# Layer norm sums taken in the eviction and on ScalarE instead of VectorE statistics, in a fused audio tower kernel

## The reference

```python
ewma = (forward EWMA + backward EWMA) / 2 over time, alpha = 0.1
h  = ewma @ tok_W.T + tok_b                      # (16, 750, 256)
xn = layernorm(h)                                # over the 256 features
for l in 0, 1:                                   # a selective scan, 64 states
    delta = softplus(xn @ Wd[l] + bd[l]); u = xn @ Wi[l] + bi[l]
    s_t = exp(-delta * softplus(A_log[l])) * s_(t-1) + delta * u
    xn  = s @ Wo[l] + bo[l] + (last state @ Ws[l] + bs[l])
h  = h + xn
xf = layernorm(h)
h  = h + silu(xf @ Gs.T) * (xf @ Us.T) @ Ds.T                   # shared, 512 hidden
       + sum over 4 of 16 experts, w_e * (silu(xf @ G_e) * (xf @ U_e)) @ D_e   # routed
layernorm(v) = (v - mean(v)) / sqrt(var(v) + 1e-5)
```

## Time and profile before

| | us |
|---|---|
| three runs | 1300.79, 1304.12, 1304.29; median 1304.12 |
| the profiled execution, whole time | 1308.71 |
| its span, first to last instruction | 1306.6 |
| PE busy | 1171.1 (90%) |
| DVE busy | 940.5 (72%) |
| ACT busy | 552.0 (42%) |
| POOL busy | 414.9 (32%) |

### The profile page before, as it was taken

The page is one execution under the profiler, slowest core; times in us unless marked ns, Lnnn a source line. Parts: engine busy times, 40 slices in busy tenths (PEclk is TensorE's granted clock), DMA queues, the critical chain, the costliest instruction groups (busy, mean ns, idle before and its releaser), DMA issues.

```text
span 1306.6 us, 24750 instructions
## 1 busy us (share of the span) xinstructions
PE 1171.1 (90%) x7477; PEld 1055.9 (81%) x7477; DVE 940.5 (72%) x2374; ACT 552.0 (42%) x899; POOL 414.9 (32%) x281
## 2 busy tenths in 40 slices
PE   3548886997999989998999889998999999999997
PEld 3437765876998779987988789977998899889997
DVE  6785898598757985889758985799668855644443
ACT  1423552461354533662355434563455343223332
POOL 2022253134131623134321623153402530353233
PEclk8556886998999999999999999999999999999999
DMA  4130021022022413122131323231221321243331
GB/s 125 33 88 17 24 64 42 28 67 75 17 53 42 104 46 57 38 58 70 31 59 30 97 54 54 42 85 33 42 64 28 94 46 36 52 107 62 54 51 19
DMA packets 88288, 71.48 MB, mean 55 GB/s; under 512 B 39671, under 2 KB 82848, under 8 KB 88168
## 3 DMA queue, kind: packets, MB, share of 16 engines
q1 hardware_dynamic: 58832, 43.30, 12.2%
q0 software_dynamic: 26832, 26.06, 11.9%
q10 hardware_dynamic: 2504, 0.55, 0.2%
HBM read 31.36 MB, written 39.34 MB: 54 GB/s over the span
## 4 chain that ended last, share of the span: by engine, by line
PE 65%; DVE 24%; issue 7%; ACT 2%; POOL 1%; another core or an unknown queue 1%; DMA 1%; DVEq 0%; POOLq 0%; ACTq 0%
PE gu_ps L1692 18%; PE gu_ps L1665 14%; PE d_ps L1768 10%; PE d_ps L1749 8%; PE ch_ps L1642 3%; PE ch_ps L1736 3%; DVE h L1188 2%; PE ch_ps L1573 2%; DVE h L1196 2%; DVE stats L1202 1%; PE ch_ps L1728 1%; DVE gu_ps L1453 1%; PE ch_ps L1603 1%; DVE h L1464 1%; PE ch_ps L1591 1%
## 5 line engine op out<-in xcount | busy, mean ns | idle before, releaser
L804 POOL DMA_INDIRECT out_dram<-block_rows,entry x99 | 158.2, 1598 | 316.4 <-ACT block_rows L944 295.7
L1692 PE MATMUL gu_ps<-gu_hi,bx_hi 128*128 x792 | 236.8, 299 | 3.2 <-issue 2.1
L1692 PE MATMUL gu_ps<-gu_lo,bx_hi 128*128 x792 | 225.7, 285 | 0.0
L1692 PE MATMUL gu_ps<-gu_hi,bx_lo 128*128 x792 | 225.7, 285 | 0.0
L932 ACT ACTIVATE hid<-gu_ps 128x512 f32<-128x512 f32 (+1 forms) x195 | 115.0, 592 | 253.9 <-PE gu_ps L1692 120.8
L785 POOL DMA_INDIRECT lists<-records,pos x96 | 135.6, 1412 | 204.1 <-DVE pos L1361 178.3
L1749 PE MATMUL d_ps<-down,hid 128*125 128x256 f32 x768 | 186.0, 386 | 0.0
L1692 PEld LDWEIGHTS gu_ps<-gu_hi,bx_hi 128*128 128x128 f32 x792 | 152.5, 193 | 9.5 <-issue 8.6
L1749 PEld LDWEIGHTS d_ps<-down,hid 128*125 128x125 f32 x768 | 141.5, 192 | 19.5 <-issue 0.3
L1692 PEld LDWEIGHTS gu_ps<-gu_hi,bx_lo 128*128 128x128 f32 x792 | 152.6, 193 | 0.9
L1692 PEld LDWEIGHTS gu_ps<-gu_lo,bx_hi 128*128 128x128 f32 x792 | 151.9, 192 | 0.0
(11 more groups left out here) (279 smaller groups left out, 2866.3 us busy)
## 6 DMA issues: line engine op xcount, KB each, us to landing
block_rows<-lists SPq DMA_DIRECT2D x99, 128.0 KB
out_dram<-h SPq DMA_DIRECT2D x24, 500.0 KB
t<-rstd_scratch SPq DMA_DIRECT2D x21, 250.0 KB, 5.4
x_in<-in_x_dram SPq DMA_DIRECT2D x8, 375.0 KB, 7.5
zt<-in_x_dram SPq DMA_DIRECT2D x7, 375.0 KB
entry<-lists SPq DMA_DIRECT2D x99, 8.0 KB, 3.2
out_dram<-block_rows,entry POOLq DMA_INDIRECT x99
lists<-records,pos POOLq DMA_INDIRECT x96
```

What stands on the lines that cost most here:

```text
L804: pool.indirect_dma_start(out=out_rows[0:there, :], out_offset=bass.IndirectOffsetOnAxis(entry[n % UE][:, ID:ID + 1].bitcast(U32), 0), in_ ...
L1692: last = pe.matmul(gu_ps[:, 2 * (g % 2) + half, q * GH:(q + 1) * GH], a[n % 2][:, k, :], w[:, k, bass.ds(of, 1), half * GH:(half + 1) * GH ...
```

## The change

- `tok` and `y`: in place of one `tensor_tensor` of 512 columns and two `bn_stats`, DVE issues two `scalar_tensor_tensor` of 256 columns, each with `accum_out` into `hsum`, the row sums of its tile.
- New steps `ln1_sq` and `ln2_sq`, one a third, on ACT: four `Square` activations with bias `hsum` (a pointer), scale -256 and `accum_out` into `hsq`. Their elementwise output is thrown away, into `fw` (ln1) or `records` (ln2). In `ln1_sq` each activation waits for the one before it; the ewma scans wait for the ln1 squares (`sq1`), `tok` and `y` for the squares of the pair before.
- `ln1_stats` and `ln2_stats` keep one `tensor_scalar` of the seven operations. For pair 0 `ln1_part` does it in two parts, 8 tiles and 4 tiles.
- Pair 0: the six `residual` steps are gone; PE adds the class row to the bank with one more matmul a tile, of one row.
- Copies out of PSUM and splits of weights (`fold` 1 and 2, `shared`) move from DVE to ACT. The wait for the token bias moves from the first preparation to `tok`.
- Positions in `CHAIN`, `EARLY` and `PREPARE` are new for some 90 entries.

The core of the diff (positions shortened):

```diff
@@ CHAIN
-    ("ewma", 1, dict(SP=-27.0, DVE=-28.5, POOL=-27.0, ACT=-27.0)),
+    ("ewma", 1, dict(SP=-27.0, DVE=-29.5, POOL=-27.0, ACT=-27.0)),
     ("tok", 0, dict(PE=-28.0, DVE=-27.5)),
     ("tok", 1, dict(PE=-27.5, DVE=-27.5)),
+    ("ln1_sq", 0, dict(ACT=-26.5)),
...
-    ("rstd_row", 0, dict(PE=-23.5, ACT=-23.0)),
-    ("spread", 0, dict(SP=-19.5)),
+    ("spread", 0, dict(SP=-21.5)),
+    ("rstd_row", 0, dict(PE=-23.8, ACT=-23.7)),
...
     ("y", (0, 1), dict(PE=-5.0, DVE=-4.5)),
-    ("ln2_stats", 0, dict(DVE=-4.5, POOL=-4.0)),
+    ("ssm_log", 1, dict(ACT=-10.0, DVE=-10.5)),
+    ("ln2_sq", 0, dict(ACT=-4.5)),
@@ ticks
-                if q and step == "rstd_row" or q == 0 and step in ("rstd_t", "spread"):
+                if q and step in ("rstd_row", "ln1_part") or q == 0 and step in (
+                        "rstd_t", "spread", "ln1_stats", "residual"):
                     continue
@@ scalar, prepare
+                elif what == "shared":
+                    act.wait_ge(S["shared_mm"], n + 1)
+                    inc(act.activation(shared_part(n)[0], shared_view(n), ACT.Copy), "shared_hi")
@@ scalar, chain
+                elif step in ("ln1_sq", "ln2_sq"):
+                    n = int(step[2]) - 1
+                    wait(act, ("tok_ev", "y_ev")[n], 6 * pair + 2 * arg + 2)
+                    wait(act, ("aggr1", "aggr2")[n], (pair + NPART - 1 if pair else 0, NT * (pair - 1) + arg + 1)[n])
...
+                    for j in range(arg * SUB, (arg + 1) * SUB):
+                        if n == 0:
+                            wait(act, "sq1", NJ * pair + j)
+                        last = act.activation(records[:, j, 0:D] if n else fw[0:TP, 0:D], h_of[pair % 2][:, j, :], ACT.Square,
+                                              bias=hsum[n][:, j:j + 1], scale=-float(D), accum_out=hsq[n][:, j:j + 1])
@@ vector, chain
                 elif step == "tok":
                     wait(dve, "tok_mm", 6 * pair + arg + 1)
+                    wait(dve, "w_tokb", 16)
...
-                    inc(dve.tensor_tensor(hv, ch(step, arg, pair)[0:TP, :].rearrange("p (j d) -> p j d", d=D),
-                                          tokb_bc[:, :].unsqueeze(1).broadcast_to([TP, 2, D]), ALU.add), "tok_ev")
-                    wait(dve, "tok_ev", 6 * pair + arg + 1)
+                    wait(dve, "sq1", NJ * (pair - 1) + 2 * arg + 2)
                     for j in range(2):
-                        inc(dve.bn_stats(stats[0][:, 2 * arg + j, :], hv[:, j, :]), "st1")
+                        last = dve.scalar_tensor_tensor(hv[:, j, :], ch(step, arg, pair)[0:TP, j * D:(j + 1) * D], 1.0,
+                                                        tokb_bc[:], ALU.mult, ALU.add,
+                                                        accum_out=hsum[0][:, 2 * arg + j:2 * arg + j + 1])
+                    inc(last, "tok_ev")
                 elif step in ("ln1_stats", "ln2_stats"):
...
-                    inc(dve.tensor_tensor(mv[n][:, :, 0], st[:, :, 1], st[:, :, 4], ALU.add), a)
...
+                        variance(var[1][:], hsq[1][:, arg * SUB:(arg + 1) * SUB], "aggr2")
@@ tensor, chain, y
+                        if pair == 0:
+
+                            wait(pe, "row_ev", 1)
+                            last = pe.matmul(bank[0:TP, n * D:(n + 1) * D], one[0:1, 0:1].broadcast_to([1, TP]),
+                                             rows[0:1, b, :], start=False, stop=True)
```

More of the change, by code:

```diff
@@ L29 @@
     ("tok", 3, dict(PE=-25.0, DVE=-25.0)),
+    ("ln1_sq", 1, dict(ACT=-25.0)),
     ("pre", (0, 0), dict(PE=-19.5, DVE=-19.5)),
-    ("split", (0, 0), dict(ACT=-13.0, DVE=-14.0)),
+    ("ln1_part", 0, dict(DVE=-24.5, POOL=-27.0)),
+    ("split", (0, 0), dict(ACT=-14.5, DVE=-14.0)),
     ("tok", 4, dict(PE=-25.0, DVE=-25.0)),
-    ("split", (0, 1), dict(ACT=-13.0, DVE=-13.0)),
     ("pre", (0, 1), dict(PE=-19.0, DVE=-18.5)),
@@ L64 @@
     ("residual", 3, dict(DVE=-4.0)),
+    ("ln2_stats", 0, dict(DVE=-4.5, POOL=-4.0)),
     ("y", (1, 1), dict(PE=-4.0, DVE=-4.0)),
+    ("ln2_sq", 1, dict(ACT=-4.0)),
     ("ln2_norm", 1, dict(DVE=-2.0, ACT=-1.5)),
@@ L131 @@
     (0, "route_marks", 0): dict(DVE=12.0),
-    (1, "list", 8): dict(POOL=19.5),
-    (1, "table", 0): dict(DVE=14.5),
+    (1, "list", 8): dict(POOL=17.5),
+    (1, "table", 0): dict(DVE=14.0),
     (0, "list", 0): dict(POOL=11.0),
-    (0, "ln1_stats", 0): dict(POOL=-26.5),
     (0, "list", 8): dict(POOL=12.5),
@@ L183 @@
     (0, "ssm_decay", 1): dict(DVE=-10.0),
-    (0, "pre", (1, 2)): dict(DVE=-12.0),
+    (0, "pre", (1, 2)): dict(DVE=-10.5),
     (0, "ssm_scan", 1): dict(DVE=-9.5),
@@ L192 @@
     (1, "residual", 5): dict(DVE=-1.5),
+    (0, "split", (0, 0)): dict(ACT=-13.5),
+    (0, "split", (0, 1)): dict(ACT=-13.5),
+    (0, "rstd_t", 0): dict(ACT=-22.0),
+    (2, "residual", 1): dict(DVE=-6.5),
+    (2, "list", 8): dict(POOL=16.0),
+    (0, "residual", 2): dict(DVE=-4.0),
+    (1, "list", 7): dict(POOL=14.5),
+    (2, "list", 0): dict(POOL=12.5),
+    (2, "route_pick", 0): dict(DVE=8.0),
+    (1, "route_pairs", 0): dict(DVE=6.5),
+    (0, "x2t", (2, 1)): dict(ACT=5.0),
+    (0, "score_exp", 0): dict(ACT=5.5),
+    (0, "rstd_row", 2): dict(ACT=-21.0),
+    (0, "ln1_part", 1): dict(POOL=-20.5),
+    (2, "list", 7): dict(POOL=15.5),
+    (0, "tok", 1): dict(DVE=-27.0),
+    (2, "ewma", 1): dict(ACT=-28.0),
+    (2, "split", (0, 0)): dict(ACT=-14.0),
+    (0, "pre", (0, 1)): dict(PE=-19.5),
+    (1, "ln1_part", 1): dict(DVE=-24.0, POOL=-20.5),
+    (1, "route_order", 0): dict(DVE=7.0),
+    (1, "rstd_row", 1): dict(PE=-21.9, ACT=-23.3),
+    (1, "rstd_row", 2): dict(PE=-20.0, ACT=-20.5),
+    (1, "rstd_row", 0): dict(PE=-22.3, ACT=-22.7),
+    (0, "tok", 3): dict(PE=-26.0),
+    (1, "ln1_sq", 2): dict(ACT=-23.0),
+    (0, "route_top", 1): dict(DVE=9.5),
 }
@@ L1576, in chain @@
                 elif step == "rstd_row":
-                    wait(pe, "rstd1", 1)
+                    wait(pe, "rstd1", sum(SUB * arg >= p for p in PARTS[:-1]))
                     for j in range(SUB):
```

288 lines of the change are left out of this document (155 added, 133 removed).

## The result

The changed kernel takes 1291.68 us (median of 4 runs, 1291.47 to 1292.31), the kernel before, on the same chip, 1302.63 (1300.79 to 1304.29): the ratio is 0.990, with a 95% interval of 0.988 to 0.992. It is faster by 11 us where 35 were forecast: inside the stated range of 1246 to 1305, outside the 1248 to 1286 that the forecast gave itself. The profiled execution took 1292.31 us with a span of 1290.3; the one shown of before took 1308.71, which is 6.1 over that median, so the two profiles differ by 16.3 us where the medians differ by 11.

A forecast was written before the change was run, and what follows sets the result against it. PE was taken as the bound on average, waiting for the chain on DVE in the early stretches. 1308.7 - 10 - 12 - 13 = 1273.7 us, about 1269 in the measure of the median; range 1246 to 1305.

The forecast's parts named there:

- Tile costs: `tok` and `y` evictions on DVE: 0.94 us a bank, saving 0.50; squares on ACT at 0.60 us each.
- Twelve [matmuls] on a PE that is idle half the time there: 0, covered by the 16.9 idle us: Pair 0's one-row matmuls on PE: no cost, hidden in PE's idle time from 76 to 112 us.
- 76 to 112 us: -10: Stage up to the first shared product: DVE loses 13 us of work, product moves from 112 to about 102 us.
- Start to 76 us: 0: Start: first eviction of `pre` 2 to 3 us late, 3 us come back before `ssm_decay`; ends -3 and +3.
- 112 to 345 us: -12: Same stage at 200 to 245 and 305 to 345 us gains 6 and 3, routing of pairs 0 and 1 gains 3.
- POOL's lists and SP's loads ... move by ticks ... 0: POOL's lists and loads of routed weights: no effect, covered by loads issued four slots ahead.
- The four steady pairs: -13: 345 to 925 us: 2.9 us `hid_lo` wait and 1.6 us of clock go, 1.2 us a pair given back.
- After 925 us PE has little idle time: 0: End of the kernel, after 925 us: no gain or loss, since PE has little idle time.
- rivals 1 and 2: Accumulator output a separate instruction on both engines, 1289 us, chance 0.17; and PE's work hiding it in steady state, 1288, 0.16.
- 3: Silu and `bx_hi` behind groups of squares on ACT make PE wait: slower, +23 us, 1327; chance 0.13.

The follow-up runs named there:

- row_dve: Changed kernel with pair 0's class row added by VectorE again instead of one-row matmuls: 0.985 of the kernel before, 1286.1 us.
- no_row: Changed kernel without the addition of pair 0's class row, nothing in its place: 0.985 of the kernel before, 1286.2 us.
- sq_short: Changed kernel with the squares of pairs 2 to 7 over 8 of their 256 columns: 0.983 of the kernel before.
- row_routed: `row_dve` with the last two preparations of routed weights moved from position 11.4 to 9.4, ahead of POOL's first list: 0.987 of the kernel before.
- after_oldpos: Changed kernel with the old step positions for pairs 1 to 7, squares' steps where the change has them: 1.009 of the kernel before, 1319.7 us.
- before_newpos: Kernel before with the changed kernel's step positions for pairs 1 to 7, without the squares' steps: 1.001 of the kernel before, 1309.4 us.
- sq_twice: Changed kernel with every square of pairs 2 to 7 computed twice on ScalarE: 1.053 of the kernel before, 1378.7 us.
- row_split: Changed kernel with pair 0's class row as two rounded parts, one fp32r matmul a tile: 0.986 of the kernel before, 1287.7 us.

## Why the prediction was right or wrong

The direction was right and the size was not. The step that failed most is the one-row matmuls of pair 0, put at 0; the second is the stretch from 112 to 345 us.

- **Tile costs: right in sign, too cautious.** An accumulating eviction is 0.42 + 0.08 us in records, and two follow each other at 0.35, so the records of a bank cover 0.77 us (592.22 to 592.99 in the changed kernel) where 0.94 was taken. 0.67 a bank was saved, not 0.50; VectorE ended at 848, not 860. Part of that is in no term: the residuals went from 43.5 to 28.8 us, where only pair 0's 5.2 had been counted, and the other 9.5 are residuals that no longer stand still beside GpSimd. Squares: 0.50 + 0.19 in records, 0.50 from one to the next where they stream and 0.63 in `ln1_sq`, where each waits for the one before it, against 0.60 taken. ACT ended at 655, not 674. These errors are on the good side and explain none of the miss.
- **"Twelve [matmuls] on a PE that is idle half the time there: 0, covered by the 16.9 idle us": wrong, the largest step.** I never priced one. They are 17.0 us of records, twelve times 1.14 us from start to start, about as much as the idle time they were to hide in, and they stand inside every bank of `y`, between its products and its eviction. A cost on the chain is not covered by idle time of the engine elsewhere. Price: 9.3 us at the first product, about 6 at the end (`row_dve`, `no_row`). The stretch from 76 to 112 us also counted the residuals as 5 us saved, and they were worth nothing: `no_row` has neither and is no faster than `row_dve`.
- **"76 to 112 us: -10": right but for that term.** Without the row on TensorE it is -8.0 (103.6 against 111.6); with it, +1.3.
- **"Start to 76 us: 0": right, and for the reasons given.** The first eviction of `pre` comes at 39.17 us, 1.1 late where 2 to 3 were expected, and `ssm_decay` at 48.30 instead of 50.27; the class row's products start at 68.31 us, 0.9 earlier than before.
- **"112 to 345 us: -12": half at best: -6.4 and -7.3 up to slot 35, or -1.2 and -2.1 by the second profile of before.** The long `tok` wait of 6.3 us fell only to 5.3. New waits took the place: `hid`, 6.5 us where it was 4.6, and `states`, 4.15, new. Two causes have a run each, both of a size near the noise of single profiles: squares on the path (`sq_short`, 3.3 to 4.2 us) and the step **"POOL's lists and SP's loads ... move by ticks ... 0"**, which was wrong by 2.7 us at its place (`row_routed`), because I asked only whether loads came late and not what POOL's work does to VectorE. The rest of the missing 5 to 11 us is not placed.
- **"The four steady pairs: -13": right, and exceeded a little: -13.4 to -17.7.** The 2.9 us waits went (11.6 us to 2.2 in the `y` products) and the clock is 1.00, as said. But the number is in part luck, since the reason given was too short: I took the relief of two banks and the scan's move as the cause, while `after_oldpos` shows that relief with the old positions gives 0 and `before_newpos` that the positions without it give 2 to 4. I had not read from the orders that `ln2_stats` moves behind its squares, nor that the 2.27 us residual ahead of `hid_lo` was standing still beside GpSimd and would stop doing so.
- **"After 925 us PE has little idle time: 0".** It gave back 4.8 us by one profile of before, 1.4 by the other. One wait of 2.23 us of the `x2t` transposes for `hid_lo`, at 1027 us, was seen; the rest is not placed.
- **The sum.** -35 forecast, -16.3 between the profiles: the start has 11 of the 19 missing, slots 0 to 35 some 6, the end 5, and the steady pairs gave 3 more than asked. By medians the miss is 24 us (11 for 35): the profile of before lies 6 us over its median, the one of after does not. The measured 1291.7 us is nearest to the 1289 and 1288 of rivals 1 and 2, and neither came true as described: that the time lies inside the stated range is their doing and not the forecast's.
- **Rivals.** 1 was half right: the accumulator read is its own instruction on both engines. The Trainium skill says it of VectorE (VectorE: DVE Perf Modes, Two Vector instructions with no wait between them), and the trace agrees; that ScalarE does the same, this trace shows. But it takes 82 ns on VectorE, mostly overlapped, not the 170 assumed for its upper bound. 2 did not occur. 3 did not occur either, but its mechanism is one step away: it named Silu and `bx_hi`, and where it strikes is `hid_hi` (`sq_twice`). Its price had an error: 7.2 us against 4.5 is 2.7 a pair and not 3.5, so +17 and 1321, still outside the range.

Of the versions tried, `row_dve` is the best that computes everything, 0.985 against 0.990; beside `row_routed` and `row_split` it can't be told apart.

## What to carry to other kernels

Price each instruction that a change adds in its own type and at the clock of its stage before calling it covered, and ask whether it stands inside the chain: idle time helps only work that nothing waits for. When a sum moves to another engine, its reader's place in the first engine's queue must move too, or the wait eats what was saved. An operation in the trace that takes three times its usual time, with no wait shown, is worth asking what ran beside it on GpSimd. An engine at 50% busy can have little room left; doubling its new work shows who depends on it.
